# The order of the steps inside a fused attention layer between two expert networks: state, beta, wo, rturn and the last shared units

## What is computed

```
x = x + 0.5 * ffn(layernorm(x))
x = x + attention(layernorm(x))
x = x + 0.5 * ffn(layernorm(x))
```

```
beta = clip(sigmoid(x @ Wg + bg), 0.8, 0.9995)
phi_q, phi_k = elu(rope(q)) + 1, elu(rope(k)) + 1
S = S * b_t + phi_k_t v_t^T ;  z = z * b_t + phi_k_t      (per token and head)
y_t = (phi_q_t S) / (phi_q_t . z + eps) ;  out = y @ Wo + bo
```

## Time and profile before

| | |
|---|---|
| median of 3 runs | 900.36 us (899.62 to 901.2) |
| the profiled execution | 901.34 us |
| its span, first to last instruction | 899.6 us |
| mean granted TensorE clock | 0.981 of full speed |
| TensorE busy | 820.8 us, 91% |
| VectorE, ScalarE, GpSimd busy | 631.6, 507.1, 539.3 us |

### The profile page before, as it was taken

One profiled execution on the slowest core, in us unless ns is written; L12 is line 12 of the kernel. 1 busy time (PEld: TensorE's weight loads), 2 busy tenths in 40 slices (PEclk: granted clock), 3 DMA queues, 4 the chain that ended last, 5 costly groups with the idle time before them and its releaser, 6 DMA issues.

```text
span 899.6 us, 26468 instructions
## 1 busy us (share of the span) xinstructions
PE 820.8 (91%) x8310; PEld 752.9 (84%) x8310; DVE 631.6 (70%) x2171; ACT 507.1 (56%) x1321; POOL 539.3 (60%) x650
## 2 busy tenths in 40 slices
PE   4778988999999977999999999997998999999998
PEld 3668887989999976788788888875998999999998
DVE  5775554777777566777778777775575877777497
ACT  5643421666666436776767668665433666666432
POOL 3475652666776416767889888776422576677300
PEclk9798999999999999999999999999999999999999
DMA  7872223544544433334446432163405355555493
GB/s 217 260 239 75 79 84 120 149 131 128 138 134 123 145 48 47 48 50 95 106 74 135 113 63 78 45 154 113 166 26 157 111 157 170 156 155 154 144 371 101
DMA packets 74739, 113.82 MB, mean 127 GB/s; under 512 B 9456, under 2 KB 57776, under 8 KB 73456
## 3 DMA queue, kind: packets, MB, share of 16 engines
q1 hardware_dynamic: 50960, 65.98, 25.2%
q0 software_dynamic: 23648, 46.17, 19.5%
HBM read 59.85 MB, written 52.26 MB: 125 GB/s over the span
## 4 chain that ended last, share of the span: by engine, by line
PE 30%; POOL 12%; issue 11%; ACT 5%; DVE 3%; DMA 3%; SPq 1%; DVEq 0%; another core or an unknown queue 0%; POOLq 0%; ACTq 0%
POOL expert_out L993 8%; PE PSA L1666 7%; PE PSA L1687 4%; PE PSA L1742 4%; POOL YIDX L988 3%; PE PSA L1543 3%; PE PSA L1719 2%; PE PSA L1711 2%; PE PSA L1724 2%; PE PSA L1733 2%; ACT MEM L1162 2%; PE PSA L1567 1%; PE PSA L1505 1%; ACT MEM L1175 1%; PE PSA L1674 1%
## 5 line engine op out<-in xcount | busy, mean ns | idle before, releaser
L993 POOL DMA_INDIRECT expert_out<-MEM,YIDX x142 | 148.8, 1048 | 99.8 <-ACT MEM L1135 97.1
L968 POOL DMA_INDIRECT expert_rows<-MEM,POSU x128 | 130.5, 1019 | 80.9 <-issue 33.5
L1609 PE MATMUL PSA<-EGUh,MEMR 128*128 x568 | 172.5, 345 | 6.1 <-issue 3.4
L1543 PE MATMUL PSA<-MEMR,SGUh 128*128 128x256 f32 x720 | 150.7, 294 | 1.9 <-issue 1.7
L1543 PEld LDWEIGHTS PSA<-MEMR,SGUh 128*128 128x128 f32 x720 | 117.1, 187 | 4.3 <-issue 3.9
L1609 PEld LDWEIGHTS PSA<-EGUh,MEMR 128*128 128x128 f32 x568 | 102.6, 188 | 9.9 <-issue 9.1
L1103 ACT ACTIVATE MEM<-PSA 128x256 f32<-128x256 f32 (+1 forms) x96 | 36.3, 382 | 125.9 <-PE PSA L1543 54.8
L1543 PE MATMUL PSA<-MEMR,SGUl 128*128 128x256 f32 x360 | 103.3, 287 | 0.9 <-issue 0.9
L1298 DVE TENSOR_TENSOR MEM<-PSA,MEM 128x256 f32<-128x256 f32 (+1 forms) x96 | 39.9, 418 | 75.5 <-ACT MEM L1103 43.4
L1609 PE MATMUL PSA<-EGUl,MEMR 128*128 x284 | 91.7, 323 | 0.0
L1122 ACT ACTIVATE MEM<-PSA 128x176 f32<-128x176 f32 x142 | 45.1, 318 | 73.9 <-PE PSA L1609 51.8
(11 more groups left out here) (189 smaller groups left out, 2345.4 us busy)
## 6 DMA issues: line engine op xcount, KB each, us to landing
MEM<-expert_rows SPq DMA_DIRECT2D x142, 130.0 KB
rows_turned<-EGUl SPq DMA_DIRECT2D x7, 1024.0 KB, 4.9
MEMR<-rows_turned SPq DMA_DIRECT2D x14, 512.0 KB, 5.9
X<-expert_out POOLq DMA_DIRECT2D x12, 512.0 KB, 5.9
X<-in_L_attn_x SPq DMA_DIRECT2D x8, 512.0 KB, 6.2
X<-in_L_attn_bo POOLq DMA_DIRECT2D x8, 512.0 KB, 9.6
expert_rows<-FILL SPq DMA_DIRECT2D x30, 130.0 KB
expert_out<-MEM,YIDX POOLq DMA_INDIRECT x142
```

The source lines that it names most:

```text
L968: pool.indirect_dma_start(out=rows_d[n.f], out_offset=bass.IndirectOffsetOnAxis(ap=POSU[:, k, i:i + 1], axis=0), in_=XN[n.xn][:, c, :], in ...
L993: pool.indirect_dma_start(out=y_d[f], out_offset=bass.IndirectOffsetOnAxis(ap=YIDX[:, j % 8:j % 8 + 1], axis=0), in_=YS[j % 3], in_offset= ...
L1543: last = mm(t[0:h, w * HALF:(w + 1) * HALF], SGU[b][:, w, k, j * P:j * P + h], XT[slot][a][:, k, hf * HALF:(hf + 1) * HALF], start=i == 0, ...
L1609: last = mm(t[:, 0:2 * HE], XGR[j % 2][a][:, k, :], EGU[b][:, bass.ds(e, 1), k, :], start=i == 0, stop=i == 3 * KD - 1)
```

## The change

Eighteen entries of the tables change, and nothing else. The diff in full:

```diff
-WHEN = dict(first_sum=-9.09, scores=-0.12, mask=0.21, select=0.34, turn_copy=-0.15, back=0.88, attend=1.2, proj=-1.99, rope=-1.53, v_copy=-1.51, rope_sum=-1.02,
-            turn=-0.5, values=0.52, ocopy=0.92, wo_turn=1.48, wo_copy=1.61, state=0.34, phi_exp=-1.02, state_sum=0.51, state_scale=1.016, state_wide=1.21,
-            wo=1.937, phi=-0.8, wo_add=2.36, tile_stats=-8.46, tile_stats2=2.518, sum=-11.646, bias=-0.24, stats=-5.43, power=-4.84, scale=-4.66, xt=-4.471,
-            xt_copy=-4.08, xt_low=-3.85, beta=-3.09, beta_tanh=-2.69, beta_decay=-2.63, decay=-2.209, decay_read=-2.06)
-WHEN2 = dict(stats=5.66, power=6.06, scale=6.34, xt=6.78, xt_copy=6.95, xt_low=6.61, gap=0.01, rout=7.09, rout_copy=7.45, rturn=7.538, top=7.88, top_tanh=8.19,
-             rank=8.63, place=8.864, scatter=9.93, every=1.08)
+WHEN = dict(first_sum=-9.0, scores=-0.12, mask=0.21, select=0.34, turn_copy=-0.15, back=0.88, attend=1.2, proj=-1.99, rope=-1.53, v_copy=-1.51, rope_sum=-1.02,
+            turn=-0.5, values=0.52, ocopy=0.92, wo_turn=1.48, wo_copy=1.61, state=0.515, phi_exp=-1.02, state_sum=0.56, state_scale=1.0, state_wide=1.21, wo=1.86,
+            phi=-0.8, wo_add=2.36, tile_stats=-8.46, tile_stats2=2.51, sum=-11.6, bias=-0.24, stats=-5.43, power=-4.84, scale=-4.66, xt=-4.36, xt_copy=-4.08,
+            xt_low=-3.85, beta=-2.487, beta_tanh=-2.3, beta_decay=-2.2, decay=-2.05, decay_read=-1.8)
+WHEN2 = dict(stats=5.66, power=6.06, scale=6.34, xt=6.56, xt_copy=6.95, xt_low=6.61, gap=0.01, rout=7.09, rout_copy=7.45, rturn=7.37, top=7.88, top_tanh=8.19,
+             rank=8.63, place=8.62, scatter=9.93, every=1.08)
...
-UNITS = dict(fill=-11.28, fill_every=1.007, after=32.92, after_every=0.26)
+UNITS = dict(fill=-11.28, fill_every=0.66, after=32.92, after_every=0.3)
```

## The result

The changed kernel takes 913.0 us (median of four runs, 911.4 to 913.3) against 900.8 for the kernel before: ratio 1.013, interval 1.0107 to 1.0152. Forecast were 905.4 us with a range of 899 to 912. The direction was right, the size was not: the time lies above the range. In a later group of runs the ratio was 1.0126 (1.0080 to 1.0173).

The account below looks back on a forecast made before the run. TensorE was taken to set the pace, GpSimd close behind. Terms -1.2+3.7+0.5+4.2-1.6-0.6 = +5.0 us on the profiled 901.3, which stands 1.0 above the median, gave 905.4 us, range 899 to 912.

Parts of the forecast that it names:

- The beta tile: Once in four attention tiles: beta's products move behind turn, a gap of 0.6 us stays ahead of back, tile 10.29 to 9.15.
- Decay's tile: Tile after beta's: decay behind the scores, v waits 0.7 us for its bank, tile 8.27 to 9.65 us.
- The plain tiles: Attention: wo fills the gap ahead of back, 0.87 to about 0.1 us; three tiles ahead of first results, -1.2 us.
- rturn: Once in four tiles: router's turn directly behind rout waits about 0.65 us for its copy; +0.1 each, +0.5 for five.
- The end of attention: Last four tiles: wo goes into gaps of up to 2.26 us ahead of back; -1.6 us net.
- The front: Ahead of attention: units run before xt(8,0), which comes 6.3 us later, beta 2.7; +4.2 us with the clock's fall.
- the term for the clock: Ahead of attention: idle times of about 4 us before beta and turn(0) cost one fall of the clock, +1.5 us.
- Behind attention: xt(23) and rout(23) move up, the 1.12 us wait ahead of rout(23) goes, rturn(23) waits 0.5; -0.6 us.
- (a): Rival: the filled gap ahead of back (9.8 us of waits) wins, 892 to 897 us; chance 0.15 together with (d).
- (c): Rival: the clock stays down in front through proj(0), turn(0) and first scores, 909 to 912 us; chance 0.15.
- (b): Rival: a draw, front +2.7 us, everything else takes itself back, 900 to 902 us; chance 0.1.
- (d): Rival: GpSimd becomes the bound in attention, only holding back a gain, about 897 us; chance 0.15 together with (a).

Follow-up runs that it names:

- e_scat: Changed kernel with two scatter entries different (10.05 and 1.04), moving the first scatter of each second-ffn tile behind state_scale on GpSimd: 886.3 us, ratio 1.0103.
- e_frontold: Changed kernel with the shared network's units ahead of attention spaced as before (fill_every 1.007 for 0.66): 885.4 us, ratio 1.0100.
- c_wo_rturn: Kernel before with two entries changed, wo 1.86 and the router's turn (rturn) 7.37: 900.2 us, ratio 0.9958.
- c_state_rturn: Kernel before with wo, rturn, state, its readers and tile_stats2 moved as in the change: 898.6 us, ratio 0.9926.
- e_statewo: Kernel before with only state, its readers and wo moved as in the change (five entries): 891.1 us, ratio 0.9942.
- e_statewo_b: Same text as e_statewo, on the kernel before, run on a chip without the lateness: 872.3 us, ratio 0.9967.
- c_best: Kernel before with state, its readers and wo moved, and the scatter's entries 10.05 and 1.04 as well: 884.1 us, ratio 1.0084.

## Why the prediction was wrong

**The beta tile, the term that failed in attention.** "The tile is 9.15" came from a chain over ScalarE (beta, its tanh, the copies, `back` at 8.1 us from the scores), and took it that beta's products end where their record ends. The chain is the right one, but with a scatter over beta's products their results came 1.4 to 1.6 us behind the record, `back` started at 9.1 to 9.4 us, and the tile took 10.1 to 10.5: some 1.15 us too little in five tiles, 5.8 us. A sign was there: before, too, the late beta tiles took 10.2 to 10.5 us (one of them stands in the earlier trace rows, 10.29) where the first took 9.25. I kept none of this in the new order. Another sign is in the reads of the scores in the trace of before. Where ScalarE had stood idle for the scores, it read them 0.14 us behind their record in all 13 tiles without a scatter over them, and 0.45 to 1.04 us behind it in the 8 tiles with one. On chips without the lateness the beta tile took 8.74, 0.4 less than I said.

The lateness isn't the whole of the miss. On a chip without it, e_scat and e_frontold, the changed kernel but for one scatter or for the units' spacing, measured 1.0103 and 1.0100, 7 to 8 us slower than before. Against the trace of before on another such chip, attention takes 2.5 us more there, the front 4.6 to 5.0 and the stage behind attention 1.4. I had 1.4, 4.2 and -0.6.

**Other terms of attention, which took part of it back.** Decay's tile: right, 9.53 for 9.65, and shown by taking its wait away. The first two pairs of tiles with beta and decay: 0.8 and 0.7 us dearer; I had 1.1 each, though the 0.3 and 0.6 that I named for it make 0.9. The plain tiles: I gave three of them 1.2 us; they gave 0.1 in sum, since two tiles with transposes behind values lost (8.56 for 8.27 in one, 8.93 in another). rturn: I charged 0.5, the six tiles with rout gave 0.5; its wait is there (0.49 us each), paid by the filled gap. The end of attention, tiles 28 to 30: 3.0 us gained where I had 1.6. Of that 1.4 is in tile 28, whose price of before was not TensorE's gap but the 2.34 us of L1289. Together +4.5 for +1.4.

**The front.** Its steps were right up to beta (6.1 for 6.3, 2.6 for 2.7); the term for the clock was mis-sized. I had 1.5 us for one fall, and nothing else between beta and the first scores. That stretch took 3.0 us more than before: 1.2 from beta to proj(0), 1.3 from there to turn(0), 0.5 to scores(0), at the lower clock in its first part and again at its end. +5.6 for +4.2. What I didn't see is that the five entries of beta cost as much there by themselves, on another path. Units alone 48.65 us, beta's entries alone 48.3, both 48.65, neither 43 to 45: each hides the other, and undoing one (e_frontold) gave nothing.

**Behind attention.** -0.6 became +5.0, the other term that failed. The step was that the wait of 1.12 us ahead of rout(23) goes when xt(23) and rout(23) move up. It didn't: rout(23) waited 1.54, and xt(23) came 27.6 us behind scores(31) as before, now waiting 1.14, as it is limited by the chain through the scaled input and not by its place. But these moves are the smaller part. c_wo_rturn and c_state_rturn leave xt(23), the ranks and the units where they were, and take 74.2 and 75.3 us, as long as the changed kernel's 75.4 and 73.4. On the chips with lateness the traces fall into two sets: with rturn at its old place 70.4 (before, twice), 71.1 and 71.5, with the new one 73.4 to 75.4. So rturn's move, for which I charged 0.65 us at rturn(22) and 0.5 at rturn(23), goes with 2 to 4 us, and wo's with 0.8: wo(30) no longer stands between `back` and wo_turn(31), and TensorE waits 1.25 us there for VectorE (L1480). Of rturn's part some 0.8 us can be seen: the copy of the last values starts 3.2 to 3.3 us behind their record with rturn's new place, 2.4 to 2.5 with the old one. The rest isn't traced. And most of it hangs on the chip: where there is no lateness, this stage takes 64.3 us before, 64.6 with wo alone and 65.7 in the kernels with all entries of the change behind attention, +1.4.

**Luck in the total.** The stages of the change missed by 10.7 us (+15.7 for +5.0). That the profiled execution missed by 7.0 only comes of its first stage, which happened to be 3.7 us shorter.

**The rivals.** (a) has its mechanism confirmed in part: the gap fell from 9.8 to 2.2 us, and with beta, decay and the front left alone it wins 0.3 to 0.7% (e_statewo, e_statewo_b, c_wo_rturn, c_state_rturn), where (a) had 0.4 to 0.9%. What I had against it, "beta's tanh now stands ahead of the copy", was right. (b), a draw, is out. (c), with 0.15, came nearest to the time, and for a part of its reason: the clock cost more than one fall. That it lies so near is luck, since (c) added 4 to 7 us in front, where only 1.4 of the miss lay. (d) didn't decide here, and did in c_best.

## What to carry to other kernels

When a gap ahead of a wait is filled by moving one step, test that step alone before the ones moved with it: here one entry of 18 carried the gain of the steady tiles, and five carried most of the loss in them. A tile that is longer than its like for no reason in the waits is a warning about that stretch; work moved into it pays the same price. And where two edits delay the same chain on different engines, undoing either shows nothing, so also try each alone on the kernel before.

## What the hardware showed

TensorE's results can come well behind the end in their record. Eight traces come from chips where the kernel before took 897 us and more. In all of them the last values were read 2.4 to 3.3 us behind their record, and in the three with the changed order of beta, its products with a scatter of GpSimd over them were read 1.3 to 1.6 us behind it. Scores that ScalarE had stood idle for were read up to 1.04 us behind theirs in tiles with a scatter over them, and in the tiles without one always 0.12 to 0.15. In the twelve traces of the three chips where it took 875 to 879, it was 0.14 us for scores, with or without a scatter, and 0.13 us at most for beta and the last values. That the scatter causes it rests on this coincidence: the kernels that moved a scatter away from beta ran only on chips without the effect, so this was not shown by experiment, and what the two kinds of chips differ in stays open.

A VectorE instruction of 0.22 us took 2.2 to 3.4 us when it met a run of GpSimd's instructions, and ended 0.07 to 0.1 us behind the third of the run (on the chips without the lateness) or the second (on those with it). The Trainium skill, SBUF — State Buffer, Who interferes with whom, says that a VectorE instruction with two inputs in SBUF contends with a GpSimd instruction that reads SBUF. The rows agree in that L1289 has two such inputs, and its end follows that of a GpSimd instruction. What stays unexplained is the order: VectorE's record begins 0.2 to 0.3 us ahead of the first of GpSimd's run (578.02 and 578.36 above), which is about the time the instruction needs, and still it was held, over two or three of GpSimd's instructions in a row.
